# The first layer of the expert network: plain fp32 matmuls in place of three rounded ones

## What is computed

```python
h_norm = layer_norm(h, rn_g, rn_b)
g = softmax(einsum('bsd,ed->bse', h_norm, router_w))
top2_w, top2_idx = top_k(g, 2)                      # of E = 4 experts
top2_w = top2_w / (sum(top2_w) + EPS_GATE)
hid = einsum('bsd,edh->bseh', h, w1)                # D = 256 -> H = 512
hid = relu(layer_norm(hid, ln_g, ln_b))
expert_out = einsum('bseh,ehd->bsed', hid, w2)      # 512 -> 256
out = sum(take(expert_out, top2_idx) * top2_w)
return layer_norm(out, on_g, on_b)
```

## Time and profile before

| | us |
|---|---|
| median of 3 runs | 563.17 |
| the three runs | 554.89, 563.17, 565.58 |
| the profiled execution, its own time | 555.7 |
| its span in the trace | 554.0 |

### The profile page before, as it was taken

How to read it: one execution, slowest core, us unless ns; L and a number is a source line. 1 busy time by engine, 2 the same in 40 slices (tenths; PEclk the granted TensorE clock), 3 DMA queues, 4 the chain that set the end, 5 groups by cost and what they waited for, 6 DMA issues and landing times.

```text
span 554.0 us, 10131 instructions
## 1 busy us (share of the span) xinstructions
PE 428.8 (77%) x3078; PEld 354.0 (64%) x3078; DVE 349.1 (63%) x1071; ACT 292.5 (53%) x655; POOL 170.2 (31%) x368
## 2 busy tenths in 40 slices
PE   4999989499893856767789839999897999999100
PEld 3789866388682745655567627878775888888100
DVE  6866578789898210323686866796674566665464
ACT  3744377388981401313444424776584777878121
POOL 2000000500000000001244584577777756655100
PEclk9999999899995865558988868999998999999755
DMA  8950200000000899946111132123224233332342
GB/s 181 225 163 30 68 10 1 0 0 2 0 1 1 223 240 230 221 102 191 40 58 59 57 113 79 53 74 97 78 76 115 68 97 96 97 112 99 120 131 72
DMA packets 51616, 50.97 MB, mean 92 GB/s; under 512 B 25672, under 2 KB 46188, under 8 KB 50156
## 3 DMA queue, kind: packets, MB, share of 16 engines
q1 hardware_dynamic: 47116, 39.70, 29.1%
q0 software_dynamic: 3552, 9.74, 4.9%
q10 hardware_dynamic: 896, 0.89, 0.6%
HBM read 35.56 MB, written 15.81 MB: 93 GB/s over the span
## 4 chain that ended last, share of the span: by engine, by line
PE 49%; DVE 14%; DMA 12%; issue 9%; POOL 8%; ACT 6%; SPq 2%; POOLq 0%; DVEq 0%; ACTq 0%
PE bank L948 8%; DMA Tb<-ssm_kernels 7%; PE bank L870 7%; PE bank L388 6%; PE bank L390 5%; PE bank L389 5%; PE bank L847 3%; DMA got_b<-expert_y 3%; POOL expert_y L678 2%; POOL sorted_x L636 2%; PE bank L939 2%; PE bank L807 2%; PE bank L864 2%; PE bank L921 1%; DVE hb L1319 1%
## 5 line engine op out<-in xcount | busy, mean ns | idle before, releaser
L948 PE MATMUL bank<-w,hr 128*128 x320 | 77.2, 385 | 4.4 <-DVE ysb L1530 4.4
L1126 ACT ACTIVATE hr<-bank,gsel 128x128 f32<-128x128 f32 x160 | 60.0, 458 | 13.4 <-PE bank L939 13.4
L948 PEld LDWEIGHTS bank<-w,hr 128*128 128x128 f32 x320 | 58.4, 193 | 12.6 <-issue 6.0
L678 POOL DMA_INDIRECT expert_y<-ysb,toid x40 | 43.4, 1085 | 36.4 <-DVE ysb L1530 26.0
L847 PE MATMUL bank<-Tb,U 68*32 68x68 f32 x1024 | 33.6, 298 | 23.6 <-DMA Tb<-ssm_kernels 18.7
L847 PEld LDWEIGHTS bank<-Tb,U 68*32 68x32 f32 x1024 | 29.7, 145 | 27.3 <-DMA Tb<-ssm_kernels 21.1
L870 PE MATMUL bank<-Wo,yT 128*128 128x256 f32 x136 | 41.0, 454 | 7.0 <-ACT yT L961 6.0
L636 POOL DMA_INDIRECT sorted_x<-x2s,slot x34 | 33.5, 986 | 33.7 <-DVE slot L1458 25.1
L1530 DVE COPY ysb<-bank 128x256 f32<-128x256 f32 x40 | 16.8, 421 | 34.3 <-PE bank L948 27.1
L870 PEld LDWEIGHTS bank<-Wo,yT 128*128 128x128 f32 x136 | 29.5, 228 | 13.7 <-ACT yT L961 8.2
L592 POOL TENSOR_TENSOR Eb<-adt,kio 128x1088 f32<-128x1088 f32 x4 | 8.0, 2030 | 98.2 <-DVE adt L1274 98.2
(11 more groups left out here) (290 smaller groups left out, 1186.5 us busy)
## 6 DMA issues: line engine op xcount, KB each, us to landing
Tb<-ssm_kernels SPq DMA_DIRECT2D x16, 680.0 KB, 8.4
xg<-sorted_x SPq DMA_DIRECT2D x40, 129.0 KB, 2.1
XI<-in_x_dram SPq DMA_DIRECT2D x12, 288.0 KB, 5.5
h0r<-h_spill SPq DMA_DIRECT2D x17, 128.0 KB, 2.1
got_a<-expert_y SPq DMA_DIRECT2D x17, 128.0 KB, 3.0
got_b<-expert_y SPq DMA_DIRECT2D x17, 128.0 KB, 4.4
out_dram<-acc SPq DMA_DIRECT2D x17, 128.0 KB
w1raw<-in_L_ffn_w_dram SPq DMA_DIRECT2D x4, 512.0 KB, 8.7
```

The source lines that it names most:

```text
L678: pool.indirect_dma_start(yd, bass.IndirectOffsetOnAxis(ap=toid[:, i % 8:i % 8 + 1], axis=0), ysb[:, i % 2, :], None).then_inc(sem(f"y_sto ...
L948: mm = pe.matmul(bank[6][:, 0:D], hr[:, i % 3, c, :], w2[:, bass.ds(expert[i], 1), c, :].rearrange("p o n -> p (o n)"), start=(c == 0), st ...
L1126: last = act.activation(hr[:, i % 3, c, :], bank[3 + i % 2][:, c * P:(c + 1) * P], ACT.Relu, scale=gsel[:, i, 0, c:c + 1], bias=gsel[:, i, ...
```

## The change

The weights of the first expert layer are no longer split: SP loads them to `w1`, and the four roundings on ACT and the four subtractions on DVE in the state-space stage are gone. The rows are no longer split: ACT copies the transposed rows to one plain fp32 buffer `bT`, whose semaphore step b2 and the next b1 now wait for, and the subtraction on DVE is gone, as is its step b1 in the table of the order. Step b2 is two plain fp32 matmuls of 512 columns in place of six passes on rounded halves. Its first block waits for the loads instead of for the split. `w2` and the small tiles behind it move to lower addresses. The order of all other steps stays.

```diff
-        w1_lo, w1_hi, w2, Wor0, ysb, before, beats, ties, ranks, lastk, etab, rowr, toid, padr = place(
-            R2, R4, ("w1_lo", [P, E, DC, HF], F32R), ("w1_hi", [P, E, DC, HF], F32R), ("w2", [P, E, HC, D]),
+        w1, w2, Wor0, ysb, before, beats, ties, ranks, lastk, etab, rowr, toid, padr = place(
+            R2, R4, ("w1", [P, E, DC, HF]), ("w2", [P, E, HC, D]),
...
-        w1raw = at("w1raw", [P, E, DC, HF], R2)
...
-            ("r1", [P, 4, D]), ("h0r", [P, 4, D]), ("xb", [P, 3, D]), ("xg", [P, 4, DX]), ("bT_hi", [P, 2, DC, P], F32R),
-            ("bT_lo", [P, 2, DC, P], F32R), ("hn", [P, 2, HF]))
+            ("r1", [P, 4, D]), ("h0r", [P, 4, D]), ("xb", [P, 3, D]), ("xg", [P, 4, DX]), ("bT", [P, 2, DC, P]),
+            ("hn", [P, 2, HF]))
...
-                    sp.dma_start(w1raw[:, q - 2], ins["L0_ffn_w1"][q - 2].rearrange("(c p) h -> p c h", p=P)).then_inc(sem("experts_in"), 16)
+                    sp.dma_start(w1[:, q - 2], ins["L0_ffn_w1"][q - 2].rearrange("(c p) h -> p c h", p=P)).then_inc(sem("experts_in"), 16)
...
-                        pe.wait_ge(sem("w1_split"), E)
+                        pe.wait_ge(sem("experts_in"), 16 * E)
...
-                        mm = split3(pe, bank[1 + i % 2][:], bT_hi[:, i % 2, dc, :], bT_lo[:, i % 2, dc, :], row(w1_hi, dc),
-                                    row(w1_lo, dc), dc == 0, dc == DC - 1)
+                        mm = pe.matmul(bank[1 + i % 2][:], bT[:, i % 2, dc, :], row(w1, dc), start=(dc == 0),
+                                       stop=(dc == DC - 1))
...
-                if v in (16, 18, 20, 22):
-                    e = (v - 16) // 2
-                    act.wait_ge(sem("experts_in"), 16 * E)
-                    copy(w1_hi[:, e], w1raw[:, e]).then_inc(sem("w1_hi"), 1)
...
-                    copy(bT_hi[:, i % 2], bank[0][:, 0:D].rearrange("p (c n) -> p c n", c=DC)
-                         ).then_inc(sem("bT_hi"), 1)
+                    copy(bT[:, i % 2], bank[0][:, 0:D].rearrange("p (c n) -> p c n", c=DC)).then_inc(sem("bT"), 1)
...
-                if v in (19, 21, 25, 27):
-                    e = (19, 21, 25, 27).index(v)
-                    dve.wait_ge(sem("w1_hi"), e + 1)
-                    dve.tensor_tensor(w1_lo[:, e], w1raw[:, e], w1_hi[:, e].bitcast(F32), ALU.subtract).then_inc(
-                        sem("w1_split"), 1)
...
-                elif kind == "b1":
-                    dve.wait_ge(sem("bT_hi"), i + 1)
-                    dve.tensor_tensor(bT_lo[:, i % 2], bank[0][:, 0:D].rearrange("p (c n) -> p c n", c=DC),
-                                      bT_hi[:, i % 2].bitcast(F32), ALU.subtract).then_inc(sem("bT"), 1)
```

More of the change, by code:

```diff
@@ L199, in build_kernel @@
         (U2,) = place(R4, R5, ("U2", [L, HC, H // HC, B]))
-        h1, x2s, yT, r1, h0r, xb, xg, bT_hi, bT_lo, hn = place(
+        h1, x2s, yT, r1, h0r, xb, xg, bT, hn = place(
             R4, R5, ("h1", [P, NT, D]), ("x2s", [P, NT, DX]), ("yT", [P, 2, HC, P]),
-            ("r1", [P, 4, D]), ("h0r", [P, 4, D]), ("xb", [P, 3, D]), ("xg", [P, 4, DX]), ("bT_hi", [P, 2, DC, P], F32R),
-            ("bT_lo", [P, 2, DC, P], F32R), ("hn", [P, 2, HF]))
+            ("r1", [P, 4, D]), ("h0r", [P, 4, D]), ("xb", [P, 3, D]), ("xg", [P, 4, DX]), ("bT", [P, 2, DC, P]),
+            ("hn", [P, 2, HF]))
         got_a, got_b, acc = place(R1, R2, ("got_a", [P, 4, D]), ("got_b", [P, 4, D]), ("acc", [P, 4, D]))
@@ L318, in build_kernel @@
             "dve": dict(out=-68.3, ln1a=-47.5, ln1b=-21.4, h1a=-14.2, x2=2.7, lg=33.6, sel=34.0, rank=44.0,
-                table=50.0, rel=47.7, wts=134.7, b1=-14.6, b2=-3.4, rs=4.5, b4=32.1, c1=-1.9, c2=22.3),
+                table=50.0, rel=47.7, wts=134.7, b2=-3.4, rs=4.5, b4=32.1, c1=-1.9, c2=22.3),
             "odd": dict(yT=21.1, xb=8.8, out=17.5, h0in=6.5, x2T=4.3, lgm=8.1, scat=-0.8, gat=18.4, fin=0.3)}
```

## The result

| | before | after |
|---|---|---|
| median, 20 runs each | 561.25 us | 568.99 us |
| lowest and highest | 554.89 to 569.82 | 561.38 to 574.78 |
| span of the profiled execution | 554.0 | 564.9 |

The ratio is 1.0155, with a 95% interval of 1.0116 to 1.0193: the change makes the kernel slower, by less than 2%.

What follows compares the result with a forecast made beforehand. DMA was taken to bound the weight preparation, TensorE the first blocks and last stage, GpSimd the middle stage. Terms of +7.1 and +1.4 us gave +8.5 us on the 563.17 us median: 571.7 us, range 562 to 577 us.

Steps and rivals of the forecast that it cites:

- The cost of b2: Expert blocks: two plain fp32 matmuls take 1.72 us where six rounded passes took 1.38, +0.34 us a block.
- Last stage: 424.4 to 505.7 us: TensorE never idle, so 21 blocks at 0.34 us cost +7.1 us in full.
- First blocks: Up to the first scatters: five longer b2, +1.7 us, less 0.3 us from DVE, giving +1.4 us.
- the slot chain: First blocks: without its row subtraction DVE reaches the slot arithmetic sooner, 0.3 us back.
- Middle stage: 352 to 418 us: 14 longer b2 are hidden behind GpSimd's work, so 0, with +4.8 us as upper end.
- the lead of 5.2 us: Middle stage: a second-layer result was put ready at 391.4 us, its scatter at 396.61, so a later TensorE still arrives first.
- the 4.8 us: Middle stage: TensorE's added work, 14 blocks at 0.34 us, against 4.5 us of its idle time.
- Smaller edits: Removed weight splits, row subtraction and hand-over on ACT and DVE were covered: 0 beyond the 0.3 us in the first blocks.
- Loads as the pace: Rival on b2: weight loads, not columns, set the pace; -0.52 us a block, -13.5 us in all; chance 0.05.
- The uncovered middle stage: Rival: TensorE's delay reaches GpSimd in the middle stage, adding 4.8 us; +13.3 us in all; chance 0.17.
- The shorter hand-overs: Rival: DVE's saved 0.42 us a block shortens the first blocks, +6.7 us in all; chance 0.12 together with weight copies.

Runs made afterwards that it cites:

- plain_part1: Kernel before with plain fp32 b2 in blocks 19 to 39 only, on the high halves, all splits kept; ratio to before 1.013.
- before again: The kernel before, unchanged, profiled once more; its blocks took 185.1 us.
- edits_only: The changed kernel with the six rounded passes back in b2, reading unsplit rows and weights; ratio to before 1.004.
- warm_early: Kernel before with two needless matmuls for each of tiles 0 to 5, in TensorE's gaps; median 558.9 us, ratio 0.998.
- after again: The changed kernel, as it was, profiled once more; median 566.27 us, ratio to before 1.008.
- plain_only: Kernel before with b2 as two plain fp32 matmuls on the high halves, all roundings and subtractions kept; ratio to before 1.022.
- plain_part0: Kernel before with plain fp32 b2 in blocks 0 to 18 only, on the high halves, all splits kept; ratio to before 1.014.
- plus_430ns: The changed kernel with one more plain fp32 matmul of 256 columns in each b2; 581.08 us, ratio to before 1.034.
- two_passes: Kernel before with b2 in two rounded high-by-high passes instead of six; 557.76 us, ratio to before 0.991.

## Why the prediction was right, and where it wasn't

- **The cost of b2.** 0.43 us a record, 1.72 us a block, +0.34: as worked out from b4. What carried it, the same products by the same kind of matmul cost the same, by columns and not by records, held to 0.01 us. The single experiments agree: the period is 4.10 us wherever b2 is plain.
- **Last stage, +7.1 us.** The 21 blocks did cost that: in plain_part1, which starts them at half clock as before does, the stage takes 6.5 to 7.0 us longer. But in after the stage grew by only 5.6 us in both pairs of profiles. The step that failed is the one by which the stage's length changes by 21 x 0.34 us and by nothing else ("none gives it back"): the stage of before began with a half-clock b4 (2.6 us in the chain instead of 1.73), and the changed kernel began it at full clock. In the five profiles with six rounded passes in the b2 ahead of block 19 and nothing filled in (before, before again, edits_only, plain_part1, warm_early) that b4 was slow each time; in the five with plain matmuls there (after, after again, plain_only, plain_part0, plus_430ns) never. I didn't have this term. It is worth -1.5 us (the first period is 428.32 - 424.37 = 3.95 us before and 432.18 - 429.73 = 2.45 us after, from b1 to b1).
- **First blocks, +1.4 us.** Measured +1.4 to +1.8 us between pairs; plain_part0 has +1.6 us. The 0.3 us from the slot chain fits edits_only (-0.2 to -0.3 us), at the edge of what the profiles tell apart.
- **Middle stage, 0.** Measured +0.3 to +0.5 us: right as a number, but the lead of 5.2 us that I argued from isn't there. I let DVE copy the result of b4 at 391.0 us; it did so at 394.98 us, behind the slot arithmetic, which left 1.2 us, 0.4 us of it slack. At all other result scatters of the stage the copy was done 3 us or more ahead. What took up the 4.8 us was mostly TensorE's own idle time, 4.5 us in the stage before and 1.15 us after; that it was just enough is partly luck. plus_430ns shows where the cover ends, by way of rank matmuls, slot arithmetic and copy.
- **Smaller edits, 0.** edits_only gained nothing in the blocks beyond the 0.3 us above; it was 1.2 us longer there, with a fall of the clock and a wait that before doesn't have.
- **The sum.** 8.5 us predicted; 6.6 to 8.0 us in the blocks, and 7.7 us between the medians; the ratio of 1.0155 gives 8.7 us. The predicted 571.7 us is 2.7 us above the measured median: the median of three runs that I started from was 1.9 us above that of twenty, and the other 0.8 us is less than what these times can tell. That the sum came this close although a term of -1.5 us was missing is partly luck.
- **The rivals.** Loads as the pace fell with the period: 4.10 us with 18 loads a block against 3.77 us with 20. This is the place where the Trainium skill (Perfetto Trace Analysis, Identifying the Most-Contended Engine) would have misled if its busy share of weight loads were read as a bound: by that share TensorE was 85% busy before and 69% after, while the stage got 6% longer. The section names a second measure, the share of peak products, which I didn't work out. It says too that the busy share of matmuls is a poor measure; here that share was 100% before and after, and the stage did last as long as its matmuls. The uncovered middle stage shows in part 0.43 us a block further on: +1.4 us there and +1.8 us up to block 19, against the 6.0 us of new work. The shorter hand-overs did not pay.

## What to carry to other kernels

Where an engine has no idle time, count the products of both forms by the rate of the nearest row: three rounded passes of 512 columns cost 0.69 us for one half of D, and the plain fp32 matmul of the same width 0.86 us, so removing 17 us of DVE work in exchange made the kernel slower. Splitting paid here because its extra work lay on engines with slack. Take the slack of a result from where its reader gets it, not from where the matmul ends: a copy that is short can stand behind other work in its engine's queue. Before pricing a percent, look for what else moves by a percent: here a stretch of matmuls with two short gaps a tile ran at either of two clocks from one execution to the next, and twelve needless matmuls in the gaps lowered the median by 4.0 us, about half of what the edit under study cost.

## What the runs showed of the hardware

- A plain fp32 matmul of 512 columns appears as two records that follow in 0.43 us each, 0.86 us a matmul; the rounded kind has one record and takes 0.23 us.
- The granted clock between 262 and 286 us was at or near 1.00 (2.4 GHz) in ten profiles (0.89 at the lowest, over 12 us of plus_430ns) and 0.50 (1.2 GHz) in two, for the same instructions, with gaps of 0.69 and 0.52 us a tile in either case; two of the ten had the gaps filled. The half-clock stretch lasted until the order of work changed near 290 us and cost 10 us. The Trainium skill (TensorE: Matmul & The Clock Gate, A second HAM failure mode: psum-queue depth-cycling) tells of a kernel whose clock swings because TensorE idles briefly and often between groups of matmuls; these traces agree in part: with the gaps filled the slow executions were gone, but eight profiles kept full clock with the same gaps, and in the other two the clock stayed at one level for over 20 us and didn't swing.
- Ahead of block 19 TensorE sat idle for 2.4 to 3.2 us in the five profiles that then fell to half clock, and for 0.9 to 2.6 us in the five with plain matmuls, which didn't. A wait of 2.38 us (before again) was followed by half clock, one of 2.62 us (after again) was not. The length of the wait alone doesn't decide, then. two_passes, which has two rounded passes there, kept full clock too, after the longest wait of all, 3.43 us. What decides stays open.
